# Queries' inverse norm moved from the query rows into the exponential, and the power split in two halves

## The reference, cut to what matters

```python
h = shift_token(x); q, k, v = split(h @ wqkv)          # 8 heads of 64
q = l2norm(q) * qs;  k = l2norm(k) * ksc               # x / max(|x|, 1e-12)
q, k = rotary_xpos(q, k)                               # linear in q and in k, row by row
sim = einsum(q * 8, k) over this and the former window of 64 keys; sim[mask] = -max
attn = softmax(sim);  out = attn @ v;  x = x + out @ wo
```

## Time and profile before

| what | value |
|---|---|
| median of three timed runs | 1995.46 us |
| span of the profiled execution (its own time) | 2052.9 us |
| TensorE busy | 1657.8 us, 81% of the span |
| ScalarE (ACT) busy | 1219.5 us, 59% |
| VectorE (DVE) busy | 1103.2 us, 54% |
| GpSimd (POOL) busy | 786.1 us, 38% |
| the 64 powers on GpSimd | 191.7 us |
| the 64 products `unit` on VectorE | 81.0 us |
| the 512 exponentials on ScalarE | 181.7 us, and 108.3 us for reading the sums |
| the 128 maxima on VectorE | 88.3 us |

### The profile page before, as it was taken

One profiled execution on the slowest core, in us unless ns is written; L12 is line 12 of the kernel. 1 busy time (PEld: TensorE's weight loads), 2 busy tenths in 40 slices (PEclk: granted clock), 3 DMA queues, 4 the chain that ended last, 5 costly groups with the idle time before them and its releaser, 6 DMA issues.

```text
span 2052.9 us, 37396 instructions
## 1 busy us (share of the span) xinstructions
PE 1657.8 (81%) x13911; PEld 1075.7 (52%) x13911; DVE 1103.2 (54%) x2039; ACT 1219.5 (59%) x2805; POOL 786.1 (38%) x654
## 2 busy tenths in 40 slices
PE   3865488887877998988887897899788895788786
PEld 2234355435665665634665664634665673456463
DVE  4124601538766545766776344665775344665573
ACT  3752266545645897477645886389555772265572
POOL 2530423326342455166225345266216223152440
PEclk7896588869988998999888998899999997789997
DMA  5000343011021432011012341011003440010110
GB/s 153 1 1 1 108 128 100 3 50 39 20 73 62 118 109 56 6 40 25 17 52 75 118 124 33 6 30 24 17 26 105 123 128 21 18 40 17 32 25 11
DMA packets 64214, 109.54 MB, mean 53 GB/s; under 512 B 12463, under 2 KB 37283, under 8 KB 63907
## 3 DMA queue, kind: packets, MB, share of 16 engines
q1 hardware_dynamic: 58339, 98.23, 16.3%
q0 software_dynamic: 4096, 8.40, 1.4%
q10 hardware_dynamic: 1600, 0.52, 0.1%
HBM read 74.40 MB, written 15.93 MB: 44 GB/s over the span
## 4 chain that ended last, share of the span: by engine, by line
PE 48%; DVE 19%; ACT 15%; issue 8%; POOL 4%; DMA 2%; another core or an unknown queue 2%; SPq 0%; ACTq 0%; DVEq 0%; POOLq 0%
PE PX L863 5%; PE PX L1256 4%; PE PX L1189 4%; PE PX L1276 4%; PE PX L1088 4%; ACT back_arena L1565 3%; PE PX L1210 3%; ACT middle_arena L1513 2%; PE PX L1099 2%; PE PX L911 2%; ACT front_arena L1400 2%; PE PX L1200 2%; PE PX L1312 2%; POOL front_arena L2270 2%
## 5 line engine op out<-in xcount | busy, mean ns | idle before, releaser
L1400 ACT ACTIVATE front_arena<-PX 128x1024 f32<-128x1024 f32 (+3 forms) x352 | 271.1, 825 | 110.5 <-PE PX L911 84.2
L2270 POOL TENSOR_TENSOR front_arena<-front_arena,tri 128x256 f32<-128x256 f32 x234 | 184.0, 801 | 358.9 <-ACT front_arena L1400 358.7
L2333 POOL TENSOR_TENSOR back_arena<-back_arena 128x512 f32<-128x512 f32 x128 | 191.4, 1501 | 320.3 <-DVE back_arena L2128 319.9
L1256 PE MATMUL PX<-wqkv,hT 128*128 128x512 f32 x384 | 217.9, 660 | 25.8 <-ACT back_arena L1565 12.4
L1565 ACT ACTIVATE back_arena<-PX,fnm 128x128 f32<-128x128 f32 x512 | 181.7, 373 | 94.2 <-DVE fnm L2135 93.2
L2338 POOL TENSOR_TENSOR fy<-fm,minus_half 128x16 f32<-128x16 f32 x64 | 191.7, 2995 | 64.8 <-DVE fm L2151 63.1
L863 PE MATMUL PX<-front_arena 128*32 128x512 f32 (+3 forms) x1408 | 172.5, 557 | 30.5 <-POOL front_arena L2270 20.8
L2135 DVE TENSOR_REDUCE fnm<-PX 128x4 f32<-128x512 f32 x128 | 88.3, 690 | 150.8 <-PE PX L1276 142.7
L911 PE MATMUL PX<-front_arena 32*128 32x512 f16 (+3 forms) x768 | 122.8, 356 | 33.3 <-ACT front_arena L1400 13.4
L1276 PE MATMUL PX<-back_arena 64*64 64x128 f32 x2048 | 143.5, 280 | 0.2 <-ACT back_arena L1603 0.2
L1276 PEld LDWEIGHTS PX<-back_arena 64*64 64x64 f32 x2048 | 111.7, 135 | 50.9 <-issue 49.8
(11 more groups left out here) (303 smaller groups left out, 3592.6 us busy)
## 6 DMA issues: line engine op xcount, KB each, us to landing
W<-in_W SPq DMA_DIRECT2D x44, 514.0 KB
middle_arena<-in_W SPq DMA_DIRECT2D x39, 514.0 KB
back_arena<-back_arena SPq DMA_DIRECT2D x128, 128.0 KB, 2.4
xpos<-x_tables SPq DMA_DIRECT2D x64, 128.0 KB, 2.0
y_rows<-middle_arena SPq DMA_DIRECT2D x20, 256.0 KB, 5.5
back_arena<-in_W SPq DMA_DIRECT2D x9, 514.0 KB
middle_arena<-x_rows SPq DMA_DIRECT2D x8, 512.0 KB, 4.4
x_tables<-back_arena SPq DMA_DIRECT2D x1, 2048.0 KB, 7.5
```

The source lines that it names most:

```text
L1256: pe.matmul(p, hT[:, 128 * i:128 * i + 128], wqkv[:, l, c:c + 512], start=True, stop=True).then_inc(filled(b, "f" + n, l, i), 1)
L1400: act.activation(pb[:, :, 0:n], p[:, :, 0:n], ACT.Exp, scale=INV_SQRT_HD).then_inc(freed(b, "S", half, g, kc, jp), 1)
L2270: pool.tensor_tensor(pb, pb, tri[:, :].unsqueeze(1).to_broadcast([128, 2, 128]), ALU.mult).then_inc(sg("masked"), 1)
L2333: pool.tensor_tensor(T1[k % 2][:, hs, :], T1[k % 2][:, hs, :], T2[:, hs, :], ALU.add).then_inc(sg("rot"), 1)
```

## The change

The power is taken in two instructions of 8 columns each: the keys' half first, into `fyk`, which signals `inverse`; then the queries' half, into one of three buffers `fyq`, which signals a new semaphore `inverse_q`. `unit` multiplies only the keys, 128 x 512. The queries stay unscaled through the transpose, and the transpose of the queries waits for the rotary step only. The scores then miss the factor of the query row, which is positive, so the maximum can be taken first and multiplied afterwards: `largest` gets a second instruction that makes `fnb` = `fnm` x factor for four heads, behind its own maximum, and only then signals `largest`. The exponential takes that as its bias and the factor, one column of `fyq`, as its scale. The mask of -1e30 is added to the unscaled scores as before.

```diff
+QRING = 3
-        fy = sb("fy", [128, 16])
+        fyk = sb("fyk", [128, NH])
+        fyq = [sb(f"fyq{i}", [128, NH]) for i in range(QRING)]
+        fnb = sb("fnb", [128, 8])
 def turn_step(b, l, t, s):
-    pe.wait_ge(sg("unit"), k + 1)
+    if s:
+        pe.wait_ge(sg("unit"), k + 1)
+    else:
+        pe.wait_ge(sg("rot"), 2 * k + 1)
 def exps(b, l, t, r):
-    ins = act.activation(fP[:, h, :], p[:, c:c + 128], ACT.Exp,
-                         bias=fnm[:, h:h + 1], accum_out=fden[:, h:h + 1])
+    head = 2 * (h - 4 * r) + r
+    ins = act.activation(fP[:, h, :], p[:, c:c + 128], ACT.Exp, bias=fnb[:, h:h + 1],
+                         scale=fyq[k % QRING][:, head:head + 1], accum_out=fden[:, h:h + 1])
 def largest(b, l, t, r):
-    dve.tensor_reduce(fnm[:, 4 * r:4 * r + 4], p, AX, ALU.max, negate=True).then_inc(sg("largest"), 1)
+    ws = slice(4 * r, 4 * r + 4)
+    dve.tensor_reduce(fnm[:, ws], p, AX, ALU.max, negate=True).then_inc(sg("peak"), 1)
+    dve.wait_ge(sg("inverse_q"), k + 1)
+    dve.wait_ge(sg("peak"), 2 * k + 1 + r)
+    dve.tensor_tensor(fnb[:, ws], fnm[:, ws], fyq[k % QRING].rearrange("p (c r) -> p r c", r=2)[:, r],
+                      ALU.mult).then_inc(sg("largest"), 1)
 def unit(b, l, t):
-    v = T1[k % 2]
-    dve.tensor_tensor(v, v, fy[:, :].unsqueeze(2).to_broadcast([128, 16, DH]), ALU.mult).then_inc(sg("unit"), 1)
+    v = T1[k % 2][:, NH:2 * NH, :]
+    dve.tensor_tensor(v, v, fyk[:, :].unsqueeze(2).to_broadcast([128, NH, DH]), ALU.mult).then_inc(sg("unit"), 1)
 def norms(b, l, t):
-        dve.wait_ge(sg("inverse"), k)
+        dve.wait_ge(sg("inverse_q"), k)
 # GpSimd, attention
-    pool.tensor_tensor(fy[:, :], fm[:, :], minus_half[:, :], ALU.pow).then_inc(sg("inverse"), 1)
+    pool.tensor_tensor(fyk[:, :], fm[:, NH:2 * NH], minus_half[:, 0:NH], ALU.pow).then_inc(sg("inverse"), 1)
+    if k >= QRING:
+        is_free(pool, *of_tile("fs", k - QRING, 1))
+    pool.tensor_tensor(fyq[k % QRING][:, :], fm[:, 0:NH], minus_half[:, 0:NH], ALU.pow).then_inc(sg("inverse_q"), 1)
```

More of the change, by code:

```diff
@@ L2134, in largest @@
                     p = read(dve, b, "fs", l, t, r).rearrange("p (h n) -> p h n", h=4)
-                    dve.tensor_reduce(fnm[:, 4 * r:4 * r + 4], p, AX, ALU.max, negate=True).then_inc(sg("largest"), 1)
+                    k = (b * DEPTH + l) * NT + t
+                    ws = slice(4 * r, 4 * r + 4)
[4 more added lines that the diff above has]
+                                      ALU.mult).then_inc(sg("largest"), 1)
                 def unit(b, l, t):
```

## The result

The changed kernel takes 2018.28 us (median of 4 runs, 2017.02 to 2019.37), the kernel before beside it 1994.67: ratio 1.0113 [1.0088, 1.0138]. It is slower by 1.1%, where the forecast was 1999 and the range ended at 2013. In a later session it was 1.0104 [1.0075, 1.0133].

What follows compares the result with a forecast made beforehand. It took the late power to set the last stretch's pace, with exponentials and five powers on the mixed stretch's chain. Mixed +5.1 and last -1.4 gave +3.7 on 1995.5: 1999 us, range 1985 to 2013.

Steps and rivals of the forecast that it cites:

- The last stretch: From 1800 to 2005 us, changed layers alone: -4.0 + 3.2 - 1.8 + 1.7 - 0.5 = -1.4 us.
- the faster rival: Exponentials' second operand column costs nothing, so a half pays 0.20 us: 1986 us, chance 0.16.
- A half pays: Each half's exponentials end 0.20 + 0.38 = 0.58 us later, for product and scale column.
- the 19 halves of the sum: Mixed stretch: two thirds of the 29 halves of exponentials on the chain, each paying 0.58 us.
- the mixed stretch: From 464 to 1700 us, beside other streams: two thirds of costs and gains, +11.2 - 6.1 = +5.1 us.
- the chain: Chain of waits in the mixed stretch: 3.3% on exponentials, 40.8 us or 29 halves, and five powers.
- 7 x 0.58: Last stretch: longer exponentials' cost of 0.58 us, set against 1.15 gained, in seven waits; net 7 x 0.57 = -4.0.
- 3.2: Last iterations of both layers: longer exponentials of three halves and two products cost 1.6 us each, 3.2 together.
- 1.7: First scores of both layers wait for TensorE, not the power: three times 0.58 = +1.7 us.
- 7 x 1.15: Last stretch: the maximum of half 1 starts 1.15 us earlier, in seven waits for the power.
- the exponentials' path decides: Slower rival: in the mixed stretch all 29 halves pay, 16.8 us, powers' gains are lost: 2014 us, chance 0.27.
- Halves not apart: Slower rival: an eight-column power beside `unit` takes much longer than 1.64 us, keys gain little: 2010 us, chance 0.07.

Runs made afterwards that it cites:

- neither: The changed kernel without the product behind the maximum and without the scale column (queries' norm left out of the exponent): 1973.01 us, 0.9879 of the kernel before.
- off_path: The changed kernel without scale column, exponentials released by the bare maximum, product still made on VectorE but unused: 1986.55 us, 0.9948 of the kernel before.
- act_off_path: The kernel before plus an unused 128 x 320 copy on ScalarE behind each half's fourth exponential: 2025.62 us, ratio 1.0112.
- half_unit: The kernel before with `unit` on the keys only, power left whole, queries left unscaled: 1984.98 us, ratio 0.9941.
- split_pool: The kernel before with the power split, keys first, and the queries multiplied on GpSimd behind their half of the power: 1994.6 us, ratio 0.998.
- before_scale_col: The kernel before with a column of ones added as scale of the exponential, nothing left out: 2028.47 us, ratio 1.0158.

## Why the prediction was wrong

**Right.** The split power, `unit`, the wait for the power, the column's 89 ns (462 - 373), the iteration of 9.78 us. The last stretch changed by -2.8 us and what follows it by +5.2 (61.7 to 66.8), together +2.4 where -1.4 was forecast. TensorE's time for its matmuls changed by as much in both, -2.9 (169.5 to 166.6) and +5.2, so the two sums bear nothing out; the second is the same 333 matmuls at a granted clock of 0.87 and 0.81:

```profile
1936.74:1998.40 61.66, 39.82 (x333) 27.82 (x331) 26.76 (x45) 23.79 (x65) 6.94 (x5) 0.87 0.05 13
1948.67:2015.50 66.83, 45.04 (x333) 30.78 (x331) 26.93 (x49) 25.22 (x65) 7.28 (x6) 0.81 0.05 12
```

The Trainium skill's page "ScalarE: Activation LUTs" (section "What ACT_TABLE_LOAD costs") gives about 93 ns for each pointer operand; these traces agree, 88 to 90 ns for the scale, and the faster rival, the free column, is out.

**Mis-sized.** The product behind the maximum takes 0.27 us with its gap, not 0.20, and the exponentials start as much later (0.30 us behind the maximum instead of 0.03). The gap of 0.03 us was read from an operation that follows a sum of squares; behind the maximum it is 0.10. A half pays 0.63 us instead of 0.58; over the 19 halves of the sum that is 1 us.

**The step that failed** is that of the mixed stretch: "3.3% of 1236 us is 40.8 us of exponentials on the chain [...] 29 halves [...] so I take two thirds: +11.2 - 6.1 = +5.1 us." Measured there, by the profiles, are +28.1 for the costs (neither to changed) and -17.8 for the gains (before to neither): +10.2, within the 12 us that were to show the prediction wrong. Each side is two and a half to three times its term. In the timings, over the whole run, the costs are 19 + 28 = 47 us and the gains 24, where the sum had 20 (11.2 + 7 x 0.58 + 3.2 + 1.7) against 16.5 (6.1 + 7 x 1.15 + 1.8 + 0.5).

Why the chain was the wrong ruler: it is one path of one execution, and the step took the number of halves on it for fixed, and cut it. The number grew instead: with the column alone the chain lies on exponentials for 70 us in place of 42, 28 us more, some 39 halves in place of 30 by the estimate above. And it counts the time that lies on that path alone. off_path and act_off_path put instructions into the lists of VectorE and ScalarE for which themselves nobody waits, and 14 of 34.6 us (128 x 0.27) and 22 of 46 us (128 x 0.36) came out all the same; half_unit took 34.6 us (64 x 0.54) away, and 12 came out. Each engine here works its list off in order, so what is added holds up all that stands behind it, of the other streams too, and some of that is late for somebody, as the keys' square behind the copy (85.4 us of waiting in place of 67.0). So the deduction "the chain counts too many" went the wrong way: with waiting for them the 46 us of columns cost 28 to 31.5, 0.6 to 0.7 of their list time, and the 34.6 us of products 19, 0.54.

Of the rivals "the exponentials' path decides" was nearest (2014): it let all 29 halves pay, 16.8 us, and the gains of the mixed stretch vanish. In fact both sides count in full and more, so that its time came close is in part luck. "Halves not apart" is refuted by the powers of 1.74 and 1.66 us. GpSimd's 0.4 us more for each tile "at nothing" was not tested by itself; split_pool's 68 us more there cost 20, so "at nothing" was too kind if these came from GpSimd's list and the same holds for 24 us.

**Left open.** Where each half hands its delay on: VectorE's wait for the keys' square takes the column's delay up (67.0 to 85.8, 61.8 to 89.6), but without that wait the time went up. How the column's cost divides between stretches: the mixed stretch took 14 to 19 us more with it in two pairs of profiles (1174.4 to 1188.0, 1160.0 to 1178.7) and 7 in the third (1177.8 to 1185.2), within what single profiles scatter. A kernel that takes away only the later end of the exponentials was not tried.

How much goes by TensorE's granted clock is open too. It is a mean of two levels, 1.2 and 2.4 GHz: 0.90 in the last stretch of before is a fifth of the time at the lower one, 0.95 in neither a tenth, 0.88 in before_scale_col a quarter, and TensorE's time for about the same matmuls was 169.5, 160.0 and 174.5 us. The timed runs of the kernel before scatter with the clock as well (a run of 1988.84 us had 0.899, one of 2004.93 had 0.889). By a line through 95 of them, 11 us less for each 0.01 more, an estimate: at equal clock some 17 us of neither's gain are left, 8 of off_path's and of half_unit's, and of the costs 20 in before_scale_col, 18 in act_off_path and 18 in the changed kernel. The order stays, but the fractions of list time given above come out at a quarter to a half, and the copy costs nearly as much as the column. Whether the clock makes part of the difference or follows from TensorE's longer waits, no run tells.

## What to carry to other kernels

Where several streams share in-order engines, price an edit first by the list time that it adds or removes on each engine, times its count. Here a third to two thirds of it came out in the end time, also where no wait names it, part of it perhaps through TensorE's clock; the chain's share before the edit gave less than half of the costs, since more of the line came onto the chain as it grew. Look at TensorE's granted clock before you compare two profiles. An operand that moves work from 64 large instructions to 512 small ones pays per instruction: 46 us of columns and 34.6 us of products stood here against 34.6 us of a halved `unit`. Try a gain without its price (neither) before pairing the two.

## What the runs showed of the hardware

A 128x4 product behind a maximum that it reads starts 0.10 us after its end, where an operation behind a sum of squares starts after 0.03; with its own 0.17 us that is 0.27 us for 512 numbers. A column as scale adds 88 to 90 ns to an exponential that already has a column as bias, whether its contents are constant or new. GpSimd's power costs by the column: 2.91 us for 16, 1.65 for 8 in the rows above (3.00, 1.74 and 1.66 on the mean); two halves cost 0.4 us more than the whole.
